# Attention stages of an eight-layer hybrid network: rows turned in the free half of the products' bank, two result buffers, the second norm on GpSimd, other places for the side products

## The reference

```python
# causal: L0_attn_b
q, k, v = heads(x @ Wq.T), heads(x @ Wk.T), heads(x @ Wv.T)
p = softmax(where(causal, q @ k.T / sqrt(8), lowest)); out = merge(p @ v) @ Wo.T
# full, twice: the first half of L1_ffn, whose input has already been through layernorm
h = X * rsqrt(mean(X * X) + 1e-6) * norm1_w
q, k, v = h @ wq, h @ wk, h @ wv            # 16 heads of 8
X = X + merge(softmax(q @ k.T / sqrt(8)) @ v) @ wo
h2 = X * rsqrt(mean(X * X) + 1e-6) * norm2_w   # goes to the router and the experts
```

## Time and profile before

| | |
|---|---|
| median of 3 runs | 2734.9 us (2730.52 to 2736.27) |
| time of the profiled execution | 2730.92 us |
| span of the profiled execution | 2729.2 us, granted clock 0.925 of full |
| PE, PEld busy | 2255.9 us, 1641.4 us |
| DVE, ACT, POOL busy | 1791.8 us, 1568.8 us, 1325.0 us |

### The profile page before, as it was taken

One profiled execution on the slowest core, in us unless ns is written; L12 is line 12 of the kernel. 1 busy time (PEld: TensorE's weight loads), 2 busy tenths in 40 slices (PEclk: granted clock), 3 DMA queues, 4 the chain that ended last, 5 costly groups with the idle time before them and its releaser, 6 DMA issues. The chain is left out here.

```text
span 2729.2 us, 65546 instructions
## 1 busy us (share of the span) xinstructions
PE 2255.9 (83%) x19720; PEld 1641.4 (60%) x19720; DVE 1791.8 (66%) x4959; ACT 1568.8 (57%) x3495; POOL 1325.0 (49%) x2493
## 2 busy tenths in 40 slices
PE   5999997999498888995978888896567778888895
PEld 3666665699365555895845555595233445555695
DVE  5667766444577775444767878566677567877566
ACT  2555554367376664575648788344255258777344
POOL 3557665455256775453234555454311334555463
PEclk9999999899599998997979999898877879999897
DMA  2000000322200003123000000224000000000224
GB/s 58 1 5 11 10 11 9 103 63 71 68 2 11 15 14 92 49 72 99 0 5 4 15 13 16 80 81 114 9 0 0 6 5 6 14 14 14 84 84 137
DMA packets 132260, 100.01 MB, mean 37 GB/s; under 512 B 23159, under 2 KB 119941, under 8 KB 132032
## 3 DMA queue, kind: packets, MB, share of 16 engines
q1 hardware_dynamic: 97088, 51.95, 7.1%
q0 software_dynamic: 18304, 36.88, 4.0%
q10 hardware_dynamic: 16640, 8.39, 1.2%
HBM read 58.22 MB, written 40.76 MB: 36 GB/s over the span
## 5 line engine op out<-in xcount | busy, mean ns | idle before, releaser
L1150 ACT ACTIVATE A_Pm<-A_t 128x768 f32<-128x768 f32 (+1 forms) x512 | 469.1, 916 | 209.4 <-PE A_t L1571 205.6
L339 POOL DMA_INDIRECT ybuf<-F_yo,F_idx x284 | 297.2, 1046 | 264.1 <-DVE F_yo L537 133.4
L1563 PE MATMUL A_s<-A_K,A_Q 32*128 32x256 f32 (+1 forms) x2640 | 326.5, 340 | 82.9 <-DVE A_mx L1351 60.2
L1351 DVE TENSOR_REDUCE A_mx<-A_s 128x4 f32<-128x1024 f32 x264 | 321.5, 1218 | 85.6 <-PE A_s L1563 78.3
L1035 POOL TENSOR_SCALAR_AFFINE_SELECT A_Pm<-A_Pm 128x256 f32<-128x256 f32 x512 | 216.9, 447 | 228.8 <-ACT A_Pm L1150 226.1
L192 POOL DMA_INDIRECT xbuf<-xs,dst x256 | 264.6, 1034 | 125.9 <-issue 60.5
L1598 PE MATMUL A_ot<-A_Pm,A_V 128*32 128x256 f32 (+3 forms) x3640 | 299.5, 394 | 25.6 <-POOL A_Pm L1035 16.6
L1563 PEld LDWEIGHTS A_s<-A_K,A_Q 32*128 32x128 f32 x2640 | 193.3, 188 | 199.9 <-issue 103.1
L1571 PE MATMUL A_t<-A_Q,A_K 32*128 32x256 f32 (+1 forms) x2560 | 306.3, 333 | 0.0
L673 PE MATMUL F_hb<-F_xT,F_wt 128*128 128x128 f32 x2272 | 303.9, 277 | 2.3 <-DVE F_wt L547 1.2
L673 PEld LDWEIGHTS F_hb<-F_xT,F_wt 128*128 128x128 f32 x2272 | 275.7, 191 | 5.6 <-ACT F_xT L378 1.9
(11 more groups left out here) (434 smaller groups left out, 5118.7 us busy)
## 6 DMA issues: line engine op xcount, KB each, us to landing
F_xr<-xbuf SPq DMA_DIRECT2D x284, 68.0 KB, 1.8
xs<-ybuf ACTq DMA_DIRECT2D x16, 512.0 KB, 11.3
xs<-ybuf SPq DMA_DIRECT2D x16, 512.0 KB, 10.0
ybuf<-F_yo,F_idx POOLq DMA_INDIRECT x284
xbuf<-xs,dst POOLq DMA_INDIRECT x256, 2.3
F_WA<-in_L_ffn_ew SPq DMA_DIRECT2D x2, 2048.0 KB, 9.4
F_WA<-in_L_ffn_ew SPq DMA_DIRECT2D x16, 256.0 KB, 5.5
F_WA<-in_L_ffn_e_gate SPq DMA_DIRECT2D x2, 1024.0 KB, 5.6
```

The lines of the kernel that those rows point to most:

```text
L339: pool.indirect_dma_start(out=YBUF[:, :], out_offset=bass.IndirectOffsetOnAxis(ap=idx[n][:, h:h + 1], axis=0), in_=yo[r][:, h, :], in_offs ...
L1150: act.activation(Pm[r][:, j:j + 2, :], tbank[:, :].rearrange("p (j k) -> p j k", j=2)[:, :, 0:PW], ACT.Exp, scale=SCALE).then_inc(t_free, 1)
L1351: last = dve.reduce_max(tops.rearrange("p t j -> p j t"), sbank[:, :].rearrange("p (j t k) -> p j t k", j=2, t=TPS), AX)
L1563: last = pe.matmul(sbank[:, k * 512 + o:k * 512 + o + nk], Q1[q][r, c + t * P:c + (t + 1) * P], K1[q][r, c:c + nk], start=not masked, stop ...
```

## The change

It does these things in A2, A4 and A5 (`split`), and leaves A1's schedule as it is:

- The normed rows of sequence b+2 are turned in the second half of `obank`, right behind `turn_back` in group 1, under one semaphore; the router's rows likewise in groups 0 and 3 of p = 1. T, RT0 and RT1 leave the list of the shared banks, which has 8 uses in every sequence. ScalarE reads the turned rows inside `context`. `xT` gets two buffers.
- `O` has two buffers, so `context` does not wait for the reader of the last result in that form.
- Side products: QK0, QK1 in group 0; QK2, QK3 in group 1; V, D in group 2; ctxT, y in group 3. `dense_low` moves from the end of the sequence to (2, 1).
- VectorE's other steps: norm at (0, 1), reciprocals at (1, 0), stat at (1, 1), context at (2, 0). In A2 `next_stat` goes to the end of the sequence.
- The second norm of A4 and A5 is one GpSimd tensor_tensor in group 1.
- `maxima` writes the high part straight into `padm` (two operations for three), and `turn_max` is a matmul of `padm` in fp32r with an fp32r identity.
- GpSimd's sends and roots change groups: `SENDS` is (1, 1, 0, 2) for full and (0, 2, 1, 1) for causal; `root` goes to group 2, A2's `next_root` to group 0.

```diff
-        order = ["QK0", "QK1", "QK2", "V", "QK3", "T", "ctxT", "y", "D"]
-        routed_order = ["RT0", "QK0", "QK1", "QK2", "V", "QK3", "T", "RT1", "ctxT", "y", "D"]
+        order = routed_order = ["QK0", "QK1", "QK2", "QK3", "V", "D", "ctxT", "y"]
...
-    SENDS = (1, 1, 2, 0) if full else (1, 0, 2, 1)
+    SENDS = (1, 1, 0, 2) if full else (0, 2, 1, 1)
+    turned_bank = obank[:, SEQ:2 * SEQ]
...
-                pool.tensor_tensor(mh[:, :, :], mx[r][:, :, :], nil8[:, :, :], ALU.add).then_inc(m_high, 1)
+                pool.tensor_tensor(padm[r][:, :, :, MROW], mx[r][:, :, :], nil8[:, :, :], ALU.add).then_inc(m_high, 1)
                 pool.wait_ge(m_high, n + 1)
-                pool.tensor_tensor(padm[r][:, :, :, MROW], mh[:, :, :].bitcast(F32), nil8[:, :, :], ALU.add)
-                pool.tensor_tensor(padm[r][:, :, :, MROW + 1], mx[r][:, :, :], mh[:, :, :].bitcast(F32), ALU.subtract).then_inc(m_split, 1)
+                pool.tensor_tensor(padm[r][:, :, :, MROW + 1], mx[r][:, :, :], padm[r][:, :, :, MROW].bitcast(F32), ALU.subtract).then_inc(m_split, 1)
+
+            def second_norm(b):
+                pool.wait_ge(xhat_ready, b + 1)
+                pool.tensor_tensor(xn[:, :, :], YS[:, b + S0, :, :], rs3[:, :].unsqueeze(2).to_broadcast([P, TPS, D]), ALU.mult).then_inc(xn_ready, 1)
...
-            def context(n, g, k):
+            def context(n, g, k, p, turned=None):
                 act.wait_ge(ob_full, n + 1)
-                if g == 0:
-                    act.wait_ge(norm_chain, k * NNORM + 3) if diff else act.wait_ge(ctx_ready, k + 1)
+                if g == 0 and diff:
+                    act.wait_ge(norm_chain, k * NNORM + 3)
+                elif g == 0 and (not isinstance(k, int) or k > 0):
+                    act.wait_ge(ctx_ready, k)
+                O = Os[1 - p if g == 3 else p]
...
+                if turned is not None:
+                    dst, scale = turned
+                    last = act.activation(dst, turned_bank, ACT.Identity, scale=scale)
                 last.then_inc(o_free, 1)
...
-                steps = {(0, 1): (next_stat,), (1, 0): (reciprocals,), (1, 1): (context, norm), (2, 1): (stat,)}
-                if full:
-                    del steps[0, 1]
+                steps = {(0, 1): (norm,), (1, 0): (reciprocals,), (1, 1): (stat,), (2, 0): (context,)}
...
+                            if split and (g, half_) == (2, 1):
+                                dense_low(use(i, p, "D"), b + 2, bank_of(i, p, "D"))
                             route_part((p, g, half_), i, starts, ends)
                     add_y(b, use(i, p, "y"), bank_of(i, p, "y"))
-                    if split:
-                        dense_low(use(i, p, "D"), b + 2, bank_of(i, p, "D"))
+                    if split and masked:
+                        next_stat(b + 1, use(i, p, "y") + 1)
...
+                    if split:
+                        last = pe.matmul(mbank[:, t * P:(t + 1) * P], wide, G["identr"][:, :], start=True, stop=True)
...
+                        if split:
+                            if g == 1:
+                                pe.wait_ge(xn_ready, b + 3)
+                                turn_back(n, xn)
+                            elif starts and p == 1 and g in (0, 3):
+                                h = 0 if g == 0 else 1
+                                pe.wait_ge(rxn_ready, 2 * (i - 1) + h + 1)
+                                turn_back(n, rxn[h])
+                            else:
+                                turn_back(n)
+                            if g == 0:
                                 project(use(i, p, "QK0"), 0, bank_of(i, p, "QK0"), lead["D1"] if isinstance(i, int) and b == 0 else use(i, 0, "D") if p else use(i - 1, 1, "D"))
+                                project(use(i, p, "QK1"), 1, bank_of(i, p, "QK1"))
+                            elif g == 1:
+                                project(use(i, p, "QK2"), 2, bank_of(i, p, "QK2"))
+                                project(use(i, p, "QK3"), 3, bank_of(i, p, "QK3"))
+                            elif g == 2:
+                                values(use(i, p, "V"), bank_of(i, p, "V"), 1 - p)
+                                pe.wait_ge(o_free, n + 1)
+                                project_dense(use(i, p, "D"), bank_of(i, p, "D"), p)
+                            else:
+                                project_out(use(i, p, "y"), bank_of(i, p, "y"), use(i, p, "ctxT"))
```

More of the change, by code:

```diff
@@ L819, in attention_stage @@
     xn = sb("xn", [P, TPS, D])
-    xT = sb("xT", [P, SEQ])
     split = not diff
+    xTs = [sb(f"xT{k}", [P, SEQ]) for k in range(2)] if split else [sb("xT", [P, SEQ])] * 2
     QT = F32R if split else F32
@@ L833, in attention_stage @@
     OT = sb("OT", [P, NS * SEQ])
-    padm = [sb(f"padm{k}", [P, TPS, QUAD, GR]) for k in range(2)]
-    O = sb("O", [P, TPS, NMAP, OV])
+    padm = [sb(f"padm{k}", [P, TPS, QUAD, GR], QT) for k in range(2)]
+    Os = [sb(f"O{k}", [P, TPS, NMAP, OV]) for k in range(2)] if split else [sb("O", [P, TPS, NMAP, OV])] * 2
     rec = sb("rec", [P, TPS, NMAP])
@@ L1023, in _ @@
             for k in range(2):
-                pool.memset(padm[k][:, :, :, :], 0.0)
+                pool.memset(padm[k][:, :, :, :].bitcast(F32) if split else padm[k][:, :, :, :], 0.0)
             pool.memset(Pm[1][:, :, :], 1.0).then_inc(p_set, 1)
@@ L1084, in _ @@
                     else:
+                        if g == 1 and full:
+                            second_norm(b + 2)
                         for k in range(SENDS[g]):
@@ L1092, in _ @@
                                 first_copy(b - 3)
-                        elif g == 1:
+                        if g == (1 if full else 0):
                             next_root(b)
-                        elif g == 3 and b + 3 < NSEQ + 2:
+                        elif g == 2 and b + 3 < NSEQ + 2:
                             root(b + 3)
@@ L1123, in take, with x_turned @@
                 act.activation(out, in_, ACT.Identity, **how).then_inc(misc_read, 1)
-            def x_turned(m, misc):
-                take(m, xT[:, :], misc[:, 0:SEQ], scale=insc[:, :] if full else 1.0)
+            def x_turned(m, misc, q=0):
+                take(m, xTs[q][:, :], misc[:, 0:SEQ], scale=insc[:, :] if full else 1.0)
             def dense(m, n, misc):
@@ L1197, in squares_of_next @@
                 last.then_inc(mv_next_ready, 1)
-            def second_norm(b):
-                act.wait_ge(xhat_ready, b + 1)
-                for t in range(TPS):
-                    last = act.activation(xn[:, t, :], YS[:, b + S0, t, :], ACT.Identity, scale=rs3[:, t:t + 1])
-                last.then_inc(xn_ready, 1)
             def pair(i, starts, ends):
@@ L1213, in pair @@
                             squares_of_next(b, offset(i, p))
-                        elif full and g == 2:
-                            second_norm(b + 2)
                         if g == 3:
@@ L1326, in _ @@
             dve.memset(V[1][:, :, :, 0:DV], 0.0).then_inc(v_step, 1)
-            dve.memset(O[:, :, :, :], 1.0)
+            for k in range(2 if split else 1):
+                dve.memset(Os[k][:, :, :, :], 1.0)
             dve.wait_ge(v_step, 1)
@@ L1436, in _ @@
                 stat(2)
+                if masked:
+                    next_stat(0, lead["T"] + 1)
             with_max(0, 0, 0)
@@ L1521, in turn, with project_dense @@
                 last.then_inc(misc_full, 1)
-            def project_dense(m, misc, turned):
+            def project_dense(m, misc, q):
                 free_bank(m)
-                pe.wait_ge(misc_read, turned + 1)
                 for n in range(2):
-                    last = pe.matmul(misc[:, n * SEQ:(n + 1) * SEQ], raw[:, n * P:(n + 1) * P], xT[:, :], start=True, stop=True)
+                    last = pe.matmul(misc[:, n * SEQ:(n + 1) * SEQ], raw[:, n * P:(n + 1) * P], xTs[q][:, :], start=True, stop=True)
                 last.then_inc(misc_full, 1)
@@ L1606, in turn_back @@
                     last = pe.transpose(obank[:, c * P:(c + 1) * P], OT[:, c * P:(c + 1) * P], ident[:, :])
+                if also is not None:
+                    for t in range(TPS):
+                        last = pe.transpose(turned_bank[:, t * P:(t + 1) * P], also[:, t, :], ident[:, :])
                 last.then_inc(ob_full, 1)
@@ L1660, in route_turn, with route_logits @@
                 last.then_inc(misc_full, 1)
-            def route_logits(turned):
-                pe.wait_ge(misc_read, turned + 1)
+            def route_logits(i):
+                if split:
+                    pe.wait_ge(o_free, i * 2 * NQ + 1)
+                else:
+                    pe.wait_ge(misc_read, use(i - 1, 1, "RT1") + 1)
                 for t in range(TPB):
```

153 lines of the change are left out of this document (86 added, 67 removed).

## The result

The changed kernel takes 2744.8 us (median of 16 runs, 2739.3 to 2755.4), the kernel before 2733.7 us on the same chip: ratio 1.0047, interval 1.0035 to 1.0058. It is 0.5% slower; the forecast was 2722 us, 0.5% faster than 2734.9.

The account below looks back on a forecast made before the run. PE, DVE and ACT were taken to run in lockstep, none full. Gains of 11 us (full stages) and 1.9 (causal), 13 in all, less 0.3 for lead-in, gave a forecast median of 2722 us, range 2696 to 2746.

Parts of the forecast that it names:

- What bounds the kernel: Three attention stages: PE, DVE and ACT in lockstep, none full; each half's next scores wait for the slowest of them.
- ceiling of 47 us: All three stages: waits for `O` (28.7 us) and the shared bank (about 18 us) at full value; not the forecast.
- Part 1: Full stage, routed sequences with p = 1 (second of a pair): a gain of 1.03 us each.
- pieces: Four consecutive stretches, a to d, of a full stage's p = 1 sequence: gains 0.70, -0.09, 0.11 and 0.31 us.
- Piece a: p = 1, group 0 to the start of group 1's second half: 7.24 us falls to 6.54, gain 0.70.
- Piece d: p = 1, last 2.11 us, PE-bound with y and D: without D falls to the floor, 1.80, gain 0.31.
- Part 2: Full stage, p = 0 (first of a pair), VectorE without rest: -0.52 + 0.86 - 0.12, a loss of 0.22 us.
- quicker `turn_max`: p = 0, group 0, where the logits make PE late: an fp32r matmul for a transpose saves 0.12 us.
- sum of the full stages: Each full stage 6 x (1.03 - 0.22) + 4 x 0.15 = 5.5 us, the two together 11 us gained.
- Part 4: Causal stage: pair gains 1.0 us in p = 1, loses 0.75 in p = 0; 1.9 us gained in all.
- `dense_low` rival: `dense_low` at (2, 1) blocks VectorE before the router's fourth step and group 3's reduction: 2747 us, chance 0.17.
- rival of the second norm: The second norm's 0.74 us on GpSimd stops VectorE as long, 24 us against 13 gained: 2746 us, chance 0.04.

Follow-up runs that it names:

- e9: Causal stage of the kernel before; full stages as changed, with the product for y done twice in the first sequence of each pair: 2720.1 us, ratio 0.9949.
- e6: Changed kernel, y done twice in first sequences of the full stages; causal stage with D, `next_stat` and GpSimd's order put back: ratio 0.9995.
- e10: Changed kernel with the product for y done twice in the first sequence of each pair, in all three stages: ratio 0.9982.
- e11: As e10, with `dense_low` one half group later, after the first reduction of group 3: ratio 0.9960.
- e13: As e11, with GpSimd's order of sends and roots put back in the causal stage: ratio 1.0003, on a chip of the slower kind.
- e14: As e9, with `dense_low` one half group later in the full stages: ratio 0.9979, on a chip of the slower kind.
- e5: The changed kernel itself, run and profiled again: ratio 1.0048.
- e15: Changed kernel with only `dense_low` moved one half group later, to group 3, and no extra matmuls: ratio 1.0061.
- e12: Kernel before, with the product for y done twice in the first sequence of each pair: ratio 1.0048.
- e1: Changed kernel, first sequence of each pair with the context's turn done twice and the product for y three times: ratio 0.9981.
- e7: Changed kernel, second sequence of each pair with the context's turn done twice and the product for y three times: ratio 1.0111.
- e2: Changed kernel with D, its two copies and its bank moved back from group 2 to the end of group 3 in every stage: ratio 1.0074.
- e8: Kernel before, with D of the first sequence of each pair cut to 32 of its 256 columns in each half: ratio 1.0018.
- e3: Changed kernel with GpSimd's order of sends and roots put back in the causal stage alone: ratio 1.0060.
- e17: The kernel before itself, run again on a chip of the slower kind: ratio 0.9999.

## Why the prediction was wrong

- **What bounds the kernel** held: the waits for `O` and for the bank are gone and other work took most of their place. The full stages, where no spell lies, are 11.6 us under before, out of the ceiling of 47 us for all three stages.
- **Part 1 held.** In e9, without a spell, a p = 1 sequence has 6.31, 4.73, 4.82 and 2.02 us for its pieces (from 1527.00, 1533.31, 1538.04, 1542.86 and 1544.88 below), so the gains are 0.93, 0.06, 0.02 and 0.09, together 1.10 us; forecast 0.70, -0.09, 0.11, 0.31, together 1.03. So the sum held in part by luck. Piece a gave more, since ACT was less late than its chain said. Piece d gave less: the scores at its end wait 0.47 us for the reduction, so VectorE was the late one there, and D's leaving was worth little.

```profile
1527.00 0.38 PE L1587 MATMUL A_s<-A_K,A_Q 32*128 32x256 f32 x2 [0.92 <-DVE A_mx L1369]
...
1533.31 0.39 PE L1587 MATMUL A_s<-A_K,A_Q 32*128 32x256 f32 x2 [0.45 <-ACT A_Pm L1154]
...
1538.04 0.39 PE L1587 MATMUL A_s<-A_K,A_Q 32*128 32x256 f32 x2 [0.87 <-ACT A_Pm L1154]
...
1542.86 0.39 PE L1587 MATMUL A_s<-A_K,A_Q 32*128 32x256 f32 x2 [0.58 <-DVE A_mx L1369]
...
1544.88 0.39 PE L1587 MATMUL A_s<-A_K,A_Q 32*128 32x256 f32 x2 [0.47 <-DVE A_mx L1369]
```

- **Part 2 was low by 0.2.** p = 0 takes 20.85 us against 20.40, a loss of 0.45 where 0.22 was forecast. VectorE's unbroken stretch grew by 0.43 (from 1531.92 to 1544.33 in the profile after, 12.41 us, against 11.98), 0.34 forecast; the wait ahead of `dense_low` is 0.28, 0.25 forecast. The 0.12 for a quicker `turn_max` is nil. The mean of the fp32r matmul in the row below, 312 ns against the transpose's 301, includes the spells; at a clock of 1.00 both take 299 ns by their mean, and the median is 306 in both. Of the profile after, 1455 to 1715 us:

```profile
L1642 PE MATMUL A_mt<-identr,A_padm 128*128 128x128 f32 x104 | 23.8, 312 | 0.0
...
L1059 POOL TENSOR_TENSOR A_xn<-Y,A_rs 128x256 f32<-128x256 f32 x13 | 8.0, 614 | 0.0
```

- **The sum of the full stages came out by luck**, where no spell lies: 300.0 us each (e6, e9, e10), 11.6 us under before together; 11 were forecast. But the kernel before has four half spells of its own there, in sequences that are 0.7, 0.6, 1.5 and 1.5 us longer than their like. Without these 4.3 us the gain is 7.3 us, a third less than forecast, and the term that was too small is the loss of p = 0 (0.45 for 0.22 in most of the twelve routed ones).
- **Part 4 failed.** The causal stage lost where 1.9 us were to be gained: e11, without a spell, is 3.8 us over before, and e13 is 2.3 over e14, which has the causal stage of before on the same chip. The signs of its parts were right and their sizes too hopeful: in e10 p = 1 gains 0.7 where no spell lies (1.0 forecast), p = 0 loses 1.0 (0.75 forecast), because the two sends cost 0.6 to 0.95 us in group 2, not 0.3. And the six sequences outside the hardware loop, of which those without a router were forecast to gain 0.1 each, lose 2.4 us together in e11, 1.3 in the first (which also starts with 2.3 us more of the low clock) and 1.2 in the last two.
- **The step that failed for the sign is the one under the sum**: each duration of TensorE was taken from rows at a clock of 1.00 and 0.99, and that the change could lower it was neither a term nor a rival. A spell costs 8.65 - 6.31 = 2.3 us, as in e5 above. With most spells gone the sign is the forecast's, though not the size: e10 is 4 us under before, not 13. In e5 the full stages are 15.4 us over the 600 without spells, for 23.6 us lost, 0.65 us for each; with the causal stage's 6.8, the 11.6 gained come out as 6.8 + 15.4 - 11.6 = 10.6 us slower, the difference of its stages from before (929.6 - 919.0).
- **The rivals.** The 2747 us of the `dense_low` rival is near the measured time, but for the wrong reason: its wait at (2, 1) costs 0.28 us in p = 0, e11 wins back 2 to 3 us in each full stage by moving it, and without the extra matmuls moving it leaves the kernel at 1.0061 (e15). The rival of the second norm is not seen: GpSimd takes 0.61 us for it, and a reduction of VectorE lasts 1.23 us as before. The rule that stood with it (the Trainium skill, SBUF — State Buffer, "Who interferes with whom") is neither borne out nor refuted: of the 32 second norms in this profile 20 run beside a reduction out of PSUM, and none beside a VectorE instruction with its inputs in SBUF. VectorE's own norm ends (1590.92 + 0.60), for one, just before GpSimd's begins (1591.60).
- The Trainium skill (TensorE: Matmul & The Clock Gate, "HAM oscillation — how this bites in real kernels") ties a halved clock to TensorE standing idle. The traces agree as far as idle time comes first and the level is 0.50; but the longest idle piece ahead of the spell shown is 1.36 us (1.72 ahead of one in A5), in a group in which TensorE does other work in between, and ahead of the spell of e12 shown above it is 0.87 us.

**Open.** Which feature of a stretch tips the clock; the same stretch does and does not in e5. Idle time filled or left in one place removed or kept spells as expected in e1, e7 and e10, and not in e2, e8, e12 and e13, where extra matmuls left 9.8 and 14.6 us lost. That the extra matmuls work by filling TensorE's idle time, and not by some other shift of the order, is argued and not shown; that the spells cost the time is shown.

## What to carry to other kernels

When a change takes TensorE's work out of a stretch that another engine bounds, cost the stretch behind it at half the clock too, as a rival; the granted clock in windows of a few us shows it, no list of waits does. Try redundant matmuls in TensorE's idle time there, before the signal and off the path, but measure each order anew: the same ones gained 0.65% in one and lost 0.5% in the other. And look at group lengths, not only at totals: GpSimd's order seemed worth nothing in e3 because 0.73 of its 0.95 us came back one group on.

## What the runs showed of the hardware

A granted clock of 0.50 for 6.7 us, or for half as long, came in kernels with no idle piece of TensorE over 1.8 us ahead of it, and one such spell costs 2.3 us (17.87 and 20.16 us in e5). TensorE's busy time in the 6.60 us before does not tell whether it comes: with 3.6 to 3.8 us busy it came at 26 of 30 boundaries (after, e5, e7), with 4.1 to 4.2 at none of 30 (e6, e9, e10), but on a slower chip with 4.27 (e13), and the half spells of the kernel before come behind 4.6 to 4.7. An fp32r matmul by an identity is no quicker than the fp32 transpose of 128 x 128 (both 299 ns at a clock of 1.00). And chips differ by 4.2% for one and the same kernel (2734 and 2850 us), the attention stages of the kernel before by 0.2 to 2.2% (e17).
